# A four-layer transformer kernel: the experts' bias mix as two 16-bit split products per tile, with finer waits and a new order in two places

## The reference, cut to what matters

```python
x = x + xattn0(layernorm(x), ctx, ctx)
x = x + ffn0(layernorm(x), W, b, A, B, gate_w, gate_b)
x = x + xattn1(layernorm(x), ctx, conv_w, bn_gamma, bn_beta)
x = x + ffn1(layernorm(x), router_weight, router_bias, expert_bias)
...
# xattn0, per channel over the 256 tokens
corr = ifft(fft(q) * conj(fft(k))).real
w, idx = top_k(corr, int(2 * log(L)))        # 11 shifts
w = softmax(w)
out = sum_i w[i] * take(v, minimum(idx[i] + pos, L - 1))
...
# ffn0
out = einsum(h, W) + b
final = rank_outputs[argmax(softmax(h @ gate_w.T + gate_b))]   # h @ A[:r].T @ B[:, :r].T, r of 8, 16, 32, 64
return out + final
...
# xattn1: the 60% largest of ctx per channel are the mask
crucial, rest = mask * h, (1 - mask) * h     # max and mean of each over the tokens, convolution, norm, gate A_S1, A_S2
return crucial * A_S1 + rest * A_S2
...
# ffn1
logits = h @ router_weight.T + router_bias   # 64 experts
scores = softmax(logits)
topk_w, topk_idx = top_k(scores, 8)
w_sum = topk_w.sum(axis=-1, keepdims=True)
w_dense = zeros(T, 64).at[arange(T), topk_idx].add(topk_w)
bias_mix = einsum('te,eh->th', w_dense, expert_bias)
return h * w_sum + bias_mix
```

## Time and profile before

| | us |
| --- | --- |
| median of 3 runs (lowest, highest) | 3401.5 (3396.3, 3411.59) |
| the profiled execution | 3404.98 |
| its span | 3403.3 |
| PE busy, instructions | 3051.6, 12866 |
| PEld busy | 1623.7 |
| DVE busy | 2730.5 |
| ACT busy | 2249.8 |
| POOL busy | 1586.0 |
| mean granted clock of TensorE, of full speed | 0.955 |

### The profile page before, as it was taken

The page is one execution under the profiler, slowest core; times in us unless marked ns, Lnnn a source line. Parts: engine busy times, 40 slices in busy tenths (PEclk is TensorE's granted clock), DMA queues, the critical chain, the costliest instruction groups (busy, mean ns, idle before and its releaser), DMA issues. The chain is left out here.

```text
span 3403.3 us, 48962 instructions
## 1 busy us (share of the span) xinstructions
PE 3051.6 (90%) x12866; PEld 1623.7 (48%) x12866; DVE 2730.5 (80%) x7110; ACT 2249.8 (66%) x5928; POOL 1586.0 (47%) x1164
## 2 busy tenths in 40 slices
PE   3999999999999986999999999989999999278887
PEld 1666666666666663444444444434444444223332
DVE  1999999999999994667968788786878878677775
ACT  6787888887878743655756657575666755475561
POOL 3898989899989872012112112211212120045465
PEclk8999999999999997999999999999999999589887
DMA  5555555555565414354736547463644645625452
GB/s 186 154 179 183 153 177 155 176 156 177 175 175 162 134 63 161 112 166 128 198 107 163 162 152 187 124 196 109 170 163 152 180 125 125 196 80 197 185 210 99
DMA packets 273905, 531.79 MB, mean 156 GB/s; under 512 B 34566, under 2 KB 134665, under 8 KB 250905
## 3 DMA queue, kind: packets, MB, share of 16 engines
q1 hardware_dynamic: 244380, 421.67, 40.3%
q10 hardware_dynamic: 18240, 71.34, 8.0%
q0 software_dynamic: 11008, 35.66, 3.1%
HBM read 400.57 MB, written 128.02 MB: 155 GB/s over the span
## 5 line engine op out<-in xcount | busy, mean ns | idle before, releaser
L1019 PE MATMUL acc<-xh,wq 128*128 128x512 f16 x4096 | 1209.0, 382 | 65.2 <-DVE xr L1677 22.0
L1019 PE MATMUL acc<-xl,wq 128*128 128x512 f16 x2048 | 759.9, 381 | 0.5 <-issue 0.5
L1244 ACT ACTIVATE unused<-c_first,minus_guess 128x256 bf16<-128x256 f32 x1024 | 505.2, 494 | 302.8 <-DVE minus_guess L1551 232.3
L1019 PEld LDWEIGHTS acc<-xh,wq 128*128 128x128 f16 x4096 | 400.0, 99 | 557.5 <-issue 47.3
L948 POOL DMA_DIRECT2D c_first<-ctx_pairs x120 | 66.4, 554 | 894.6 <-DVE mk L1602 880.2
L1019 PEld LDWEIGHTS acc<-xl,wq 128*128 128x128 f16 x2048 | 201.1, 98 | 244.1 <-issue 4.7
L423 PEld LDWEIGHTS bu<-m_iz,zf 128*128 128x128 f32 x2048 | 282.4, 193 | 51.7 <-issue 37.7
L423 PE MATMUL bu<-m_iz,zf 128*128 128x128 f32 (+2 forms) x2048 | 296.9, 304 | 6.5 <-POOL zf L272 6.5
L442 PE MATMUL bx<-m_ic,pf 128*128 128x256 f32 x1024 | 240.1, 388 | 10.8 <-POOL pf L336 10.8
L442 PEld LDWEIGHTS bx<-m_ic,pf 128*128 128x128 f32 x1024 | 192.5, 193 | 40.2 <-POOL pf L336 11.6
L1226 ACT ACTIVATE unread<-cf 128x256 bf16<-128x256 f32 x256 | 106.1, 414 | 138.6 <-DVE feat_pair L1650 98.3
(11 more groups left out here) (337 smaller groups left out, 7048.3 us busy)
## 6 DMA issues: line engine op xcount, KB each, us to landing
wq<-w_split SPq DMA_DIRECT2D x512, 256.0 KB, 3.2
x_first<-x SPq DMA_DIRECT2D x16, 2048.0 KB, 7.7
c_first<-ctx SPq DMA_DIRECT2D x64, 512.0 KB, 7.0
xt<-xT SPq DMA_DIRECT2D x64, 512.0 KB
x_pairs<-xo SPq DMA_DIRECT2D x64, 512.0 KB, 3.3
c_first<-ctx_pairs POOLq DMA_DIRECT2D x128, 256.0 KB, 4.5
x<-xn_pairs SPq DMA_DIRECT2D x32, 1024.0 KB, 6.5
out_pairs<-ost SPq DMA_DIRECT2D x32, 1024.0 KB, 4.8
```

Of the source, the lines that this page charges most:

```text
L1019: return pe.matmul(acc[b][:], ws[(WQ * o + k // CK) % WR][:, k % CK, a, :], x[:, k, :], start=start, stop=False)
L1244: act.activation(signs[:, u // 2, t] if n == COUNTS - 1 else unused[u % 2][:], ct[k % CR][:, t], ACT.Sign, bias=guess[q % 2][:, u:u + 1], ...
```

## The change

Three parts, independent of each other.

**Attention.** VectorE's wait for all four pieces of `kf` is split: the patched row needs the copies of slots 0 and 2, the first product also slot 1, the second product the fourth piece.

**Feed-forward.** On TensorE `gates(0)` waits only for the first of the five set-up results (`aug_ok`), tile 2 for four of them and `correct` for all. On VectorE and ScalarE the work ahead of the first pair is in another order. All eight pairs are written out, without a loop. The token means are stored as `means3`, four values to a partition.

**Experts.** The table is kept twice in 16-bit form: `e_hi` holds the rounded table in rows 0 to 63 and again in rows 64 to 127, `e_lo` what the rounding left, with two constant rows (`C_ROW`) below. The weights are put side by side twice before the transpose (`wd[:, q, 0, :]` and `wd[:, q, 1, :]`), so that `w_both` holds them rounded on rows 0 to 63 and, after `low_weights` has subtracted the rounded value, the remainder on rows 64 to 127. A tile is then `e_hi` x `w_both` plus `e_lo` x `w_hi`, both 16-bit. The token term -mean * r * w_sum + old mean is made per token on VectorE (`c_sum`), split into two parts (`c_parts`), transposed, and copied into rows 64 and 65 of `w_hi`. r * w_sum is spread over the partitions by four products with the identity instead of one with `pick`. The factors used for scaling are undone in the output (`DOWN`), which becomes a three-operand instruction. The pairs are written out here too, and `biases(0, 1, 2)` stand behind the logits of chunk 2.

```diff
@@ -664,12 +664,15 @@
-                    dve.wait_ge(k_sb, f + 1)
+                    dve.wait_ge(k_part, 3 * f + 2)
...
-                    products(bx[:], kf[s], pq, p_mul)
+                    dve.wait_ge(k_part, 3 * f + 3)
+                    dve.tensor_tensor(pq[:, 0:2, :], bx[:], kf[s][:, 0:2, :], ALU.mult).then_inc(p_mul, 1)
+                    dve.wait_ge(k_sb, f + 1)
+                    dve.tensor_tensor(pq[:, 2:4, :], bx[:], kf[s][:, 1:3, :], ALU.mult).then_inc(p_mul, 1)
...
+            for i in range(NPAIR):
+                pair(i, i % 2, i // 2)
...
+                elif o == 2:
+                    pe.wait_ge(aug_ok, OT // OG)
...
+                        pe.wait_ge(aug_ok, OT // OG + 1)
...
-                    pe.wait_ge(aug_ok, OT // OG + 1)
+                    pe.wait_ge(aug_ok, 1)
...
             moments(0, 1)
+            variance2(0)
+            first_guess(0, 1)
+            tokens(0, 0)
+            mask_second(0, GT)
             mask_step(0, 0, 0, GT)
-            first_guess(0, 1)
-            mask_second(0, GT)
-            variance2(0)
-            tokens(0, 0)
             mask_first(0, GT + 1)
...
-                sp.dma_start(wds[s][A:B, :], rows3[0:1, bass.ds(i, 1), :].rearrange("r a t -> r (a t)")).then_inc(m3_in[s], 16)
+                sp.dma_start(m3[s][:], means3[bass.ds(i, 1), :, :].rearrange("a p q -> p (a q)")).then_inc(m3_in[s], 16)
...
+                elif k == 1:
+                    pe.wait_ge(a1_ok, i)
+                pe.matmul(po[(KT * s + k) % RING][:], e_hi[:, k * P:(k + 1) * P], w_both[s][:], start=True, stop=False)
+                pe.matmul(po[(KT * s + k) % RING][:], e_lo[:, k * P:(k + 1) * P], w_hi[s][:], start=False, stop=True).then_inc(bias_mm, 1)
...
-                    mm = pe.transpose(rw_ps[0:A, q * P:(q + 1) * P], wd[:, q, :], ident[:])
+                    mm = pe.transpose(rw_ps[:, q * P:(q + 1) * P], wd[:, q, :, :].rearrange("p h e -> p (h e)"), ident[:])
                 mm.then_inc(wt_mm, 1)
-                pe.wait_ge(wds_ok, i + 1)
-                pe.matmul(rw_ps[:], pick[0:A, :], wds[s][0:A, :], start=True, stop=True).then_inc(ab_mm, 1)
+                pe.wait_ge(rw_ok, i + 1)
+                for q in range(QT):
+                    mm = pe.matmul(rw_all[:, q * P:(q + 1) * P], rw[:, q:q + 1].broadcast_to([P, P]), ident[:], start=True, stop=True)
+                mm.then_inc(ab_mm, 1)
+                pe.wait_ge(ex_ok, 2 * (i + 1))
+                for q in range(QT):
+                    mm = pe.transpose(parts[0:A, q * P:(q + 1) * P], ex[:, 2 * q:2 * q + A], ident[:])
+                mm.then_inc(ex_mm, 1)
...
-                biases(0, 1, 2)
                 squares(i, 1)
                 logits(i, s, 2)
+                biases(0, 1, 2)
                 biases(3, 4, 5)
...
+                if not least(i, 1):
+                    act.wait_ge(k_in, 64)
+                    act.activation(e_hi[:], eb, ACT.Copy, scale=B_UP).then_inc(e_hi_ok, 1)
...
+                act.activation(wd[:, :, 1, :], wd[:, :, 0, :], ACT.Copy).then_inc(wd2_ok, 1)
...
-                act.activation(wds[s][0:A, :], rw_ps[0:A, :], ACT.Copy).then_inc(wds_ok, 1)
+                act.activation(w_both[s][:], rw_ps[:], ACT.Copy, scale=W_UP).then_inc(both_ok, 1)
...
+                act.activation(w_hi[s][0:E, :], w_both[s][0:E, :], ACT.Copy).then_inc(wds_ok, 1)
+                act.wait_ge(ex_mm, i + 1)
+                act.activation(w_hi[s][E:A, :], po[(KT * s + 2) % RING][E:A, :], ACT.Copy).then_inc(wds_ok, 1)
...
-                dve.tensor_tensor(o, o, po[(KT * s + k) % RING][:], ALU.add).then_inc(out_ok, 1)
+                dve.scalar_tensor_tensor(o, po[(KT * s + k) % RING][:], DOWN, o, ALU.mult, ALU.add).then_inc(out_ok, 1)
...
+                dve.wait_ge(both_ok, i)
+                dve.scalar_tensor_tensor(w_both[s][E:P, :], rw_ps[E:P, :], W_UP, w_both[s][E:P, :], ALU.mult, ALU.subtract).then_inc(low_ok, 1)
...
-                dve.tensor_tensor(rw[:], r4[:], ws[:], ALU.mult).then_inc(step_ok, 1)
...
-                dve.tensor_copy(wd[:, :, E + 1], rw[:]).then_inc(step_ok, 1)
...
-                dve.scalar_tensor_tensor(wd[:, :, E], mean[:], -1.0, rw[:], ALU.mult, ALU.mult).then_inc(wd_ok, 1)
+                dve.tensor_tensor(rw[:], r4[:], ws[:], ALU.mult).then_inc(rw_ok, 1)
...
+                dve.scalar_tensor_tensor(cs[:], mean[:], -1.0, rw[:], ALU.mult, ALU.mult).then_inc(step_ok, 1)
...
+                dve.tensor_tensor(cs[:], cs[:], m3[s][:], ALU.add).then_inc(step_ok, 1)
...
+                dve.tensor_scalar(c16[:], cs[:], C_UP, None, ALU.mult).then_inc(step_ok, 1)
...
+                dve.tensor_copy(ex2[:, :, 0], c16[:]).then_inc(ex_ok, 1)
+                dve.scalar_tensor_tensor(ex2[:, :, 1], cs[:], C_UP, c16[:], ALU.mult, ALU.subtract).then_inc(ex_ok, 1)
...
                 x3(i, s, u, 4)
+                if least(i, 1):
+                    low_weights(i, 1 - s)
                 x3(i, s, u, 5)
...
+                    dve.scalar_tensor_tensor(e_lo[0:E, :], eb[0:E, :], B_UP, e_hi[0:E, :], ALU.mult, ALU.subtract).then_inc(e_lo_ok, 1)
```

137 lines of the change are left out of this document (70 added, 67 removed).

## The result

The changed kernel takes 3345.6 us (3343.78 to 3352.45, four runs) where the kernel before took 3402.35 beside it (3396.3 to 3411.59): ratio 0.9841, 95% interval 0.9817 to 0.9865, 57 us less. The forecast was 3374 with a range of 3350 to 3402. Its profiled execution took 3344.23.

What follows compares the result with a forecast made beforehand. Three barrier-separated stages add: attention bound by TensorE and VectorE alike, the last stage by waits and low clock. From the 3401.5 us median, -20 - 3 - 2 + 3 + 3 - 9.5 = -28.5 gave 3373, stated as 3374; range 3350 to 3402.

Steps and rivals of the forecast that it cites:

- the prediction's own signs of being wrong: Whole forecast: wrong if attention moves less than 10 us or a pair of the experts leaves 47 to 53 us.
- Attention, -20: Attention: finer VectorE waits for kf save 1.3 us in each of 16 four-step rounds; -20 us, bounds 0 and -45.
- something else ends last in each: Attention: 0.7 us is not saved in every step; the four kinds gain 0, 0.6, 0 to 0.1 and 0.7.
- rival C: Attention: ScalarE binds every step, so the 20 us are gone and the kernel takes 3394 us; chance 0.12.
- Pairs written out, -2: Feed-forward: loop pairs last 198 us, the straight-line pair 196; 2 us less for all, bounds 0 and -8.
- First pair, -3: Feed-forward, first pair: TensorE's 7.53 us wait goes, an 8 us wait comes before tile 4; -3 us, bounds 0 and -11.
- Experts' start, +3: Experts' start: e_hi adds 1.9 us, table loads 1.1, e_lo lies in VectorE's wait; +3 us, bounds +1 and +5.
- Experts' pairs, +3: Experts' pairs: 47.4 us at full clock, 50.0 with one slow burst; six times 0.5 is +3 us, bounds -13 and +63.
- I take one: Experts' pairs: one more slow-clock burst per pair, since the 2 us wait is nearer 2.73 than none; 50.0 us.
- rival A: Experts' pairs: the clock holds, 47.4 us a pair, 3358 us in all; chance 0.15.
- 52.6 a pair: Experts' pairs by the skill page's rule: both new waits bring slow bursts, +19 us for the stage instead of +3.
- The end, -9.5: Experts' end: the last tiles get shorter, POOL ends last, last output at 3389.0 instead of 3398.6; -9.5 us.

Runs made afterwards that it cites:

- a_pool_after: Changed kernel with POOL making the sum pf ahead of the split of the weights in attention: 3332.4 us, ratio 0.9820.
- a_pool_before: Kernel before with only POOL's sum pf moved ahead of the split of the weights in attention: 3397.6 us, ratio 1.0000.
- f_flat_vector: Kernel before with token means packed, plus VectorE's feed-forward pairs alone written out, other engines keeping the loop: 3368.2 us, ratio 0.9907.
- f_order_after: Changed kernel with VectorE's and ScalarE's old order ahead of the first feed-forward pair, TensorE's finer waits kept: 3349.5 us, ratio 0.9861.
- four_moves: Changed kernel with POOL's pf and ScalarE's w_back earlier, tiles 0 to 2 before chunk 2, table loads on their own semaphore, e_lo later: 3307.6 us, ratio 0.9738.

## Why the prediction was wrong

The steps that made the time come out below the range are three: the pairs written out, sized at 2 us, the packed means, which had no term, and the pairs of the experts, forecast longer and measured shorter. Attention failed the other way and hid some 11 us of it, which was luck. One of the prediction's own signs of being wrong came true, attention moving by less than 10 us; the other, a pair of the experts outside 47 to 53, only in the last one, which had been outside before as well.

- **Attention, -20, measured -8.6** (-5 between the means of all profiles with and without the finer waits). The step that failed is "something else ends last in each": the four kinds of step were weighed against ScalarE alone. In three kinds of four POOL's row ended within 0.1 us of the moment when TensorE was done with VectorE's weights, its rows stood in the trace, and it was not read. It is rival C's outcome with POOL in ScalarE's place. a_pool_after and a_pool_before show it.
- **Pairs written out, -2, measured -19 in the feed-forward stage** (13 in the whole time, 7.5 to 19.4) **and some 6 in the experts.** The term compared the loop's 198 us with a straight pair of 196. That straight pair held the 4.86 us issue, so the comparison was with a disturbed one; in six kernels with before's code there it took 190.6 to 197.5, rising with the length of that issue. The other straight pair stood in the trace with 191.3. What the loop costs VectorE's row was not counted; f_flat_vector shows that it is there.
- **Token means, no term, measured -11.** The edit was read as one of the last stage's inputs; a price was on ScalarE's queue in the stage that stores them.
- **First pair, -3:** right, with its mechanism: -2.6, the wait 7.93 for 8. By f_order_after the gain comes from the new order on VectorE and ScalarE, and the finer waits alone give none.
- **Experts' start, +3, measured +6.6.** `e_lo` was said to lie in VectorE's wait. It stood ahead of the routing, behind TensorE's transposes, for 3.2 us; TensorE's first sums waited 1.7 us longer for the table's loads, where 1.1 was taken; and the 1.2 us of the gate chain beside POOL's clearing of `e_lo` had no term. four_moves takes 7.2 back by moving the first two.
- **Experts' pairs, +3, measured -14.4.** The row of times was right to 0.7 us up to chunk 3, and the new waits came where they were said to. What failed is "I take one": one slow burst in each pair was taken, after a wait of 1.8 us, by the nearest row of 2.73, and priced at 2.6 us. The clock held in five of seven, and where it didn't the burst cost 1.5. That is rival A, held for 0.15. The sum was also off at its other end: the last six intervals of before are 48.7 us in the mean and not 49.5, so its own 50.0 a pair meant +8, and 47.4 a pair -8. Measured are 47.0 in the mean, -10.2, and -4.2 in the first interval, which had no term. Part of the gain is the written-out pairs', above. The Trainium skill's page "TensorE: Matmul & The Clock Gate", section "HAM oscillation — how this bites in real kernels", describes short bursts that start slow each time behind waits longer than the two new ones here. The prediction put its rule on these two and got 52.6 a pair; the trace has 47.4 to 48.3. For the long waits of the pair, 4.5 to 4.7 us ahead of the burst behind the third x3 step, the trace agrees: 5.0 to 6.7 us each time instead of 3.65.
- **The end, -9.5, measured -9.4:** right.

## What to carry to other kernels

When a wait of one engine is shortened, line up the rows of all engines at the point where they meet, and subtract no more than the distance to the second. A step that stays the same length under a real edit has a second row of equal length; undo that row's order and the gain appears. Compare a loop's length only with several passes outside it, and look for register instructions in the stream of the engine that TensorE waits for: most of them run beside other work, but what shows delays that engine's results. A stage that only stores something small can pay for its pieces on the queue that issues them. Before an order is changed together with the work itself, ask for each alone: here the order took back 15.8 us of what the mix gave.
